# A transformer layer on one core: a new written-out order of work, with first and last rounds in an order of their own

## The reference

```
xn = layernorm(x)
Q, K, V = xn W_Q + b_Q, xn W_K + b_K, xn W_V + b_V       # 16 heads of 64
attn    = softmax(Q K^T / sqrt(64))                      # 256 x 256 for each head
x1 = x + layernorm(sum over heads (attn V) W_O + b_O)
gate = softmax(x1n gate_w^T), x1n = layernorm(x1)        # 8 experts
f  = x1n weight^T + (1/16) sum_e gate_e (x1n U_e^T) V_e^T  # rank 16 each
out = x1 + layernorm(f)
```

## Time and profile before

| what | value |
|---|---|
| median of 3 runs | 1220.18 us |
| profiled execution | 1221.85 us, its span 1220.0 us |
| PE busy | 1185.9 us, 97% of the span, 10532 matmuls |
| DVE, ACT, POOL busy | 958.6, 967.9 and 728.3 us |
| granted TensorE clock, mean | 0.99 of 2.4 GHz |

### The profile page before, as it was taken

One profiled execution on the slowest core, in us unless ns is written; L12 is line 12 of the kernel. 1 busy time (PEld: TensorE's weight loads), 2 busy tenths in 40 slices (PEclk: granted clock), 3 DMA queues, 4 the chain that ended last, 5 costly groups with the idle time before them and its releaser, 6 DMA issues.

```text
span 1220.0 us, 32981 instructions
## 1 busy us (share of the span) xinstructions
PE 1185.9 (97%) x10532; PEld 977.1 (80%) x10532; DVE 958.6 (79%) x2618; ACT 967.9 (79%) x3079; POOL 728.3 (60%) x946
## 2 busy tenths in 40 slices
PE   6899999999999999999999999999999999999995
PEld 3688888888888888888888888888888888888883
DVE  4677888887888887887877878877888878788883
ACT  2678888888888888888888888888888888888882
POOL 2556556665556665566665666675556665555653
PEclk9899999999999999999999999999999999999997
DMA  6000000000000000000000000000000000000000
GB/s 213 2 1 6 2 6 4 4 4 4 0 4 4 4 4 4 0 4 4 4 4 4 4 0 4 4 4 4 4 0 4 4 4 4 4 0 4 4 4 9
DMA packets 9923, 10.95 MB, mean 9 GB/s; under 512 B 816, under 2 KB 9392, under 8 KB 9904
## 3 DMA queue, kind: packets, MB, share of 16 engines
q1 hardware_dynamic: 9904, 10.70, 2.7%
HBM read 6.50 MB, written 4.19 MB: 9 GB/s over the span
## 4 chain that ended last, share of the span: by engine, by line
PE 82%; POOL 7%; DVE 6%; issue 4%; ACT 1%; POOLq 0%; DVEq 0%; DMA 0%; SPq 0%; ACTq 0%
PE o_ps L383 17%; PE st_ps L365 17%; PE st_ps L355 14%; PE extra_ps L398 8%; PE qk_ps L304 4%; PE qk_ps L306 4%; PE qk_ps L305 4%; POOL probs L1021 3%; PE extra_ps L337 3%; PE extra_ps L339 2%; PE extra_ps L338 2%; DVE probs_t L806 2%; PE extra_ps L270 2%; POOL xn L1010 1%; POOL xn L1015 1%
## 5 line engine op out<-in xcount | busy, mean ns | idle before, releaser
L1021 POOL TENSOR_TENSOR probs<-probs,inv_sum 128x512 f32<-128x512 f32 x512 | 525.4, 1042 | 352.6 <-DVE inv_sum L801 342.0
L563 ACT ACTIVATE probs<-st_ps,neg_max 128x256 f32<-128x256 f32 x1024 | 475.2, 482 | 102.6 <-DVE neg_max L794 99.7
L794 DVE TENSOR_REDUCE neg_max<-st_ps 128x2 f32<-128x512 f32 x512 | 332.0, 680 | 48.8 <-PE st_ps L355 45.7
L365 PE MATMUL st_ps<-ident,probs 128*128 128x128 f32 x2048 | 286.6, 275 | 6.7 <-POOL probs L1021 5.1
L365 PEld LDWEIGHTS st_ps<-ident,probs 128*128 128x128 f32 x2048 | 233.9, 141 | 46.9 <-POOL probs L1021 21.6
L383 PE MATMUL o_ps<-probs_t,v_sb 128*64 128x256 f32 x2048 | 256.3, 387 | 0.3 <-DVE o_lo L812 0.2
L563 ACT ACTIVATION_READ_ACCUMULATOR probs<-st_ps,neg_max 128x1 f32 x1024 | 217.1, 212 | 0.0
L806 DVE COPY probs_t<-st_ps 128x512 f32<-128x512 f32 x256 | 169.4, 683 | 37.4 <-PE st_ps L365 37.3
L383 PEld LDWEIGHTS o_ps<-probs_t,v_sb 128*64 128x64 f32 x2048 | 133.4, 136 | 73.2 <-issue 5.9
L778 DVE TENSOR_TENSOR qk_lo<-qk_ps,qk_hi 128x512 fp32r<-128x512 f32 x256 | 175.1, 684 | 11.8 <-ACT qk_hi L550 11.5
L571 ACT COPY probs_t<-st_ps 128x512 f32<-128x512 f32 x256 | 152.5, 596 | 32.6 <-PE st_ps L365 32.6
(11 more groups left out here) (116 smaller groups left out, 2073.4 us busy)
## 6 DMA issues: line engine op xcount, KB each, us to landing
out<-x_all SPq DMA_DIRECT2D x32, 128.0 KB, 1.7
x_all<-in_x SPq DMA_DIRECT2D x1, 3840.0 KB, 17.3
stage_v<-in_w_v SPq DMA_DIRECT2D x1, 512.0 KB, 4.1
stage_o<-in_w_o SPq DMA_DIRECT2D x1, 512.0 KB, 6.7
stage_q<-in_w_q SPq DMA_DIRECT2D x1, 384.0 KB, 4.7
stage_k<-in_w_k SPq DMA_DIRECT2D x1, 384.0 KB, 5.8
x_all<-in_x SPq DMA_DIRECT2D x2, 128.0 KB, 3.1
ffn<-in_ffn_w SPq DMA_DIRECT2D x1, 196.0 KB, 6.8
```

The costliest lines, as they stand in the source:

```text
L365: last = nc.tensor.transpose(st_ps[p % 2][h][:, s * T + j * P:s * T + (j + 1) * P], probs[p % N_PROBS][h][:, j, s * P:(s + 1) * P], ident[ ...
L563: last = nc.scalar.activation(probs[n][h][:, j, :], st_ps[p % 2][h][:, j * T:(j + 1) * T], ACT.Exp, bias=neg_max[n][h][:, j:j + 1], accum_ ...
L794: nc.vector.tensor_reduce(neg_max[p % N_PROBS][h][:, :], st_ps[p % 2][h][:, :].rearrange("p (j s) -> p j s", j=NT), AX.X, ALU.max, negate= ...
L1021: nc.gpsimd.tensor_tensor(probs[n][h][:, :, :], probs[n][h][:, :, :], inv_sum[n][h][:, :].unsqueeze(2).to_broadcast([P, NT, T]), ALU.mult) ...
```

## The change

It does these things:

- A new order of the calls in `body` on all four engines. On TensorE a round becomes: scores 6, values 2, values 3; scores 7; scores 0, values 4, values 5; scores 1; a transposes call, then values 6, values 7, scores 2; scores 3 (between output projections 1 and 2); scores 4, values 0, values 1; scores 5, with 128*128 work between these groups. The last `project_v` moves behind `transpose_x1`.
- The first three rounds and what follows the loop are no longer `body` with holes, but lists of their own (145 calls on TensorE ahead of the loop, 26 behind it). The loop still runs 29 rounds.
- v is no longer centred by TensorE. Its column sums give `v_offset`, and v's bias goes through the output projection into the bias b_O (`output_bias`: 9 matmuls of one column; `ffn_means`: 8 matmuls of one column instead of one). `MEANS` has 6 pieces instead of 8, and POOL builds no diagonals for v.
- 12 warm-up matmuls of 128x128 at the start, and a small ScalarE copy of `one` before the weights.
- On DVE `stats_x(2)` now stands in the first list between `fold_means(3)` and `fold_means(4)`.

```diff
+WARM_UPS = 12
@@
         def run(engine, lag, body):
-            for i in range(lag + 1):
-                body(i)
             with engine.Fori(0, B - 1 - lag) as step:
                 body(step + (lag + 1))
-            for i in range(B, B + lag):
-                body(i)
@@ TensorE
+            def warm_up():
+                for _ in range(WARM_UPS):
+                    nc.tensor.matmul(st_ps[1][1][:, 0:P], mean_w[:, :], mean_w[:, :], start=True, stop=True)
+            def ffn_means():
+                pe.wait_ge(mean_folded, 5)
+                pe.wait_ge(ffn_rows_centred, 1)
+                nc.tensor.matmul(o_ps[:, 0:D + TG], mean_w[:, :], ffn[:, F_W:F_W + D + TG],
+                                 start=True, stop=True)
+                pe.wait_ge(w_loaded["v"], 16)
+                for pair in range(PAIRS):
+                    last = nc.tensor.matmul(o_ps[:, D + TG + pair:D + TG + pair + 1],
+                                            stage["v"][:, pair_cols(pair)], one[:, 0:1],
+                                            start=True, stop=True)
+                last.then_inc(ffn_means_projected, 1)
+            def output_bias():
+                ...
+                nc.tensor.matmul(dst, neg_mean_w[:, :], bias[:, B_O:B_O + 1], start=True, stop=False)
+                for pair in range(PAIRS):
+                    last = nc.tensor.matmul(dst, stage["o"][:, pair_cols(pair)], v_offset[:, pair:pair + 1],
+                                            start=False, stop=(pair == PAIRS - 1))
@@ TensorE, the first list, its beginning
+            warm_up()
+            weight_means(0)
+            transpose_xn(0)
+            weight_means(1)
+            weight_means(2)
+            project_v(0, 0, free=(xt_lo_ready, 1))
+            weight_means(3)
+            project_qk(0, 0)
+            weight_means(4)
+            project_qk(0, 1)
+            weight_means(5)
+            project_v(0, 1, free=(v_copied[0], 1))
+            ffn_means()
+            project_v(0, 2, free=(v_copied[1], 1))
+            scores(0, 0)
+            scores(0, 1)
+            project_qk(0, 2, free=(qk_lo_ready, 1))
+            project_qk(0, 3, free=(qk_lo_ready, 2))
+            output_bias()
+            transpose_probs(0, 0, 0, free=(exp_ready[0], 1))
+            ...
@@ TensorE, body(i) (the waits left out here: each call has its free= as in the list above)
+                transpose_xn(i)
+                scores(i - 1, 6)
+                probs_v(i - 1, 2); probs_v(i - 1, 3)
+                project_tg(i - 2)
+                project_qk(i, 0)
+                transpose_probs(i - 1, 5, 1); transpose_probs(i - 1, 5, 0)
+                project_qk(i, 1)
+                transpose_probs(i - 1, 6, 0)
+                scores(i - 1, 7)
+                project_v(i, 0)
+                project_qk(i, 2)
+                transpose_probs(i - 1, 6, 1)
+                project_qk(i, 3)
+                project_v(i, 1)
+                scores(i, 0)
+                probs_v(i - 1, 4); probs_v(i - 1, 5)
+                project_qk(i, 4)
+                transpose_u(i - 2)
+                transpose_probs(i - 1, 7, 0); transpose_probs(i - 1, 7, 1); transpose_probs(i, 0, 0)
+                project_z(i - 2)
+                scores(i, 1)
+                transpose_probs(i, 0, 1)
+                probs_v(i - 1, 6); probs_v(i - 1, 7)
+                scores(i, 2)
+                project_v(i, 2)
+                transpose_probs(i, 1, 0)
+                project_qk(i, 5)
+                transpose_probs(i, 1, 1)
+                output_projection(i - 1, 0); output_projection(i - 1, 1)
+                scores(i, 3)
+                output_projection(i - 1, 2)
+                transpose_probs(i, 2, 1)
+                output_projection(i - 1, 3)
+                transpose_probs(i, 2, 0)
+                project_qk(i, 6)
+                transpose_y(i - 1)
+                scores(i, 4)
+                probs_v(i, 0); probs_v(i, 1)
+                project_qk(i, 7)
+                transpose_x1(i - 1)
+                transpose_probs(i, 3, 0); transpose_probs(i, 3, 1)
+                project_v(i, 3)
+                transpose_probs(i, 4, 1); transpose_probs(i, 4, 0)
+                scores(i, 5)
@@ DVE, the first list, its beginning
+            stats_x(0)
+            norm_first_x()
+            stats_x(1)
+            fold_means(0)
+            weight_lo("v", every, w_hi_ready, w_lo_ready)
+            fold_means(1)
+            weight_lo("q", early, early_hi_ready, early_lo_ready)
+            xt_low(0)
+            weight_lo("k", early, early_hi_ready, early_lo_ready)
+            fold_means(2)
+            w_o_means()
+            centre_ffn_rows()
+            fold_means(3)
+            stats_x(2)
+            fold_means(4)
+            qk_lo(0, 0)
+            weight_lo("q", late, w_hi_ready, w_lo_ready)
+            weight_lo("o", every, w_hi_ready, w_lo_ready)
+            fold_means(5)
+            qk_lo(0, 1)
+            centre_ffn_columns()
+            weight_lo("k", late, w_hi_ready, w_lo_ready)
+            row_max(0, 0, 0)
+            ...
@@ TensorE, behind the loop, its end
+            probs_v(31, 6, free=(o_lo_ready, 127))
+            transpose_probs(31, 7, 0, free=(exp_ready[0], 256))
+            output_projection(31, 0, free=(z_copied, 31))
+            output_projection(31, 1)
+            output_projection(31, 2)
+            probs_v(31, 7)
+            output_projection(31, 3)
+            transpose_y(31, free=(yt_ready, 32))
+            ...
```

More of the change, by code:

```diff
@@ L307, in project_qk, with project_v @@
                 last.then_inc(qk_projected, 1)
[L308 to L328, removed]
+            def project_v(b, quarter, free=None):
                 if first(b) and quarter == 0:
@@ new lines, in _ @@
+            project_qk(1, 3, free=(qk_lo_ready, 10))
+            probs_v(0, 4, free=(o_lo_ready, 2))
+            probs_v(0, 5)
+            transpose_probs(0, 6, 0, free=(exp_ready[0], 7))
+            transpose_probs(0, 6, 1, free=(exp_ready[1], 7))
+            transpose_probs(0, 7, 0, free=(exp_ready[0], 8))
+            project_v(1, 2, free=(v_copied[1], 2))
+            transpose_probs(0, 7, 1, free=(exp_ready[1], 8))
+            scores(1, 0, free0=(probs_t_copied[0], 7), free1=(probs_t_copied[1], 7))
@@ new lines, in _ @@
+            project_qk(1, 7, free=(qk_lo_ready, 14))
+            probs_v(1, 0, free=(o_lo_ready, 4))
+            probs_v(1, 1)
+            scores(1, 4, free0=(probs_t_copied[0], 11), free1=(probs_t_copied[1], 11))
+            transpose_x1(0, free=(x1_ready, 1))
+            transpose_probs(1, 3, 1, free=(exp_ready[1], 12))
+            project_v(1, 3, free=(x1t_ready, 1))
+            transpose_probs(1, 3, 0, free=(exp_ready[0], 12))
+            probs_v(1, 2, free=(o_lo_ready, 5))
+            probs_v(1, 3)
@@ new lines, in _ @@
+            transpose_probs(1, 4, 1, free=(exp_ready[1], 13))
+            transpose_probs(1, 4, 0, free=(exp_ready[0], 13))
+            transpose_xn(2, free=(v_copied[3], 2))
+            scores(1, 5, free0=(probs_t_copied[0], 12), free1=(probs_t_copied[1], 12))
+            scores(1, 6, free0=(probs_t_copied[0], 13), free1=(probs_t_copied[1], 13))
+            probs_v(1, 4, free=(o_lo_ready, 6))
+            project_tg(0, free=(xt_lo_ready, 3))
+            project_qk(2, 0, free=(qk_lo_ready, 15))
@@ new lines, in _ @@
+            transpose_probs(2, 0, 1, free=(exp_ready[1], 17))
+            project_v(2, 2, free=(z_copied, 1))
+            probs_v(1, 6, free=(o_lo_ready, 7))
+            probs_v(1, 7)
+            scores(2, 2, free0=(probs_t_copied[0], 17), free1=(probs_t_copied[1], 17))
+            project_qk(2, 5, free=(qk_lo_ready, 20))
+            project_qk(2, 6, free=(qk_lo_ready, 21))
+            output_projection(1, 0, free=(v_copied[2], 3))
+            transpose_probs(2, 1, 0, free=(exp_ready[0], 18))
@@ new lines, in _ @@
+            probs_v(2, 0, free=(o_lo_ready, 8))
+            probs_v(2, 1)
+            transpose_probs(2, 3, 1, free=(exp_ready[1], 20))
+            transpose_x1(1, free=(x1_ready, 2))
+            transpose_probs(2, 3, 0, free=(exp_ready[0], 20))
+            project_v(2, 3, free=(x1t_ready, 2))
+            transpose_probs(2, 4, 1, free=(exp_ready[1], 21))
+            transpose_probs(2, 4, 0, free=(exp_ready[0], 21))
+            scores(2, 5, free0=(probs_t_copied[0], 20), free1=(probs_t_copied[1], 20))
@@ L685, in _ @@
-            run(act, 2, body)
+            nc.scalar.copy(seen_one[:, :], one[:, :])
+            weight_hi("v", every, w_hi_ready)
+            weight_hi("q", early, early_hi_ready, 1)
+            xt_high(0)
+            weight_hi("k", early, early_hi_ready, 2)
+            copy_v(0, 0)
+            qk_hi(0, 0)
+            weight_hi("q", late, w_hi_ready, 4)
+            weight_hi("o", every, w_hi_ready)
+            qk_hi(0, 1)
+            copy_v(0, 1)
+            weight_hi("k", late, w_hi_ready, 6)
@@ new lines, in _ @@
```

(17 more changed lines are left out.)

1089 lines of the change are left out of this document (717 added, 372 removed).

## The result

The changed kernel took 1232.61 us (median of 4 runs, 1232.06 to 1233.45) against 1220.13 us for the kernel before (4 runs, 1218.62 to 1221.35). The ratio is 1.0103, with a 95% interval of 1.0086 to 1.0121: slower by 12.5 us. The forecast was 1229.0, range 1219 to 1240.

The account below looks back on a forecast made before the run. TensorE's own sequence was taken to bound the loop, with waits mattering only at both ends. Median 1220.18 us, plus 14.8 (loop), minus 6 (ahead), 0 (behind), gave 1229.0 us; range 1219 to 1240.

Parts of the forecast that it names:

- The loop, +14.8 forecast: 29 loop rounds, each +0.78 us for 20 changes of shape instead of 16 and -0.27 for a removed wait for POOL.
- the places without a row: In the loop, scores before a projection (three times, 0.20 us each) and values 7 before scores 2 (0.19).
- the 0.12 of the loop's edge: Last transposes to values: 0.92 us in a loop round, 0.80 in a written-out one; the 0.12 was forecast to stay.
- the places that I called even to within 0.2 us: In the loop, project_v(i, 3) behind copy_x1t, transposes 3/0 and norm_x behind POOL: priced 0, range 0 to 0.3 us a round.
- rival 1: New waits in the loop: one place late by 0.3 us each round, +8.7 us, 1238 us; chance 0.17.
- Ahead of the loop, -6 forecast: Stretch before the loop: 4.6 us and 3.5 us gained, 2.0 lost to 11 more shape changes; from -2 to -14.
- Its first half: Ahead of the loop: load lands at 22.9, first row maximum 30.1, first transposes about 34.4 against 38.27; 4.6 us gained.
- The second half, 3.5 us from better filled rounds 1 and 2: Ahead of the loop, behind the first transposes: better filled rounds win 3.5 us of idle time and low clock.
- Behind the loop, 0 forecast: After the loop: some 2 us won, against uncovered copies behind values 7 and seven more shape changes; 0, give or take 1.5.
- 2 (the ends gain 14 us): Both ends gain all they can, load hidden or early, holes filled: +14.8 - 14 = +0.8, 1221 us; chance 0.12.
- 3 (unshown places are free): In the loop, four places no loop row shows cost nothing, 0.8 us off each round; with ends -14, 1206 us; chance 0.07.
- 4 (the surcharge hides a wait): Shape-change surcharge is time TensorE waits anyway; the loop only loses its wait: -14, 1206 us; chance 0.04.

Follow-up runs that it names:

- Experiment 1: Kernel before with project_qk(i, 1) moved between scores 6 and scores 7: 1249.68 us, ratio 1.0233.
- experiment 2: Kernel before with project_qk(i, 1) between scores 6 and 7 and project_qk(i, 6) between scores 4 and 5: 1249.35 us, ratio 1.0236.
- values_in_twos: Kernel before with values 0 moved right ahead of values 1, behind scores 4 and 5: 1230.42 us, ratio 1.0078.
- xn_ahead: Kernel before with transpose_xn moved ahead of transpose_probs(i, 4, 0): 1213.18 us, ratio 0.9936.
- experiment 9: Kernel before with an unused tile of 32 bytes a partition behind `one`, no instruction changed: 1224.45 us, ratio 1.0021.
- 3: Kernel before with values 0 moved right ahead of values 1, the same run as values_in_twos: 1230.42 us, ratio 1.0078.
- 6: Changed kernel with transpose_probs(i, 0, 1) moved ahead of scores(i, 1): 1260.42 us, ratio 1.0331.
- 11: Kernel before with transpose_xn ahead of transpose_probs(i, 4, 0), values 0 beside values 1, project_v(i, 3) and project_qk(i, 6) ahead of transposes: 1235.32 us, ratio 1.011.
- transpose_ahead: Changed kernel with transpose_probs(i, 0, 1) moved ahead of scores(i, 1), the same run as 6: 1260.42 us, ratio 1.0331.
- no_warm_up: Changed kernel without the 12 warm-up matmuls: 1231.92 us.
- experiment 8: Changed kernel with stats_x(2) later, transpose_probs(i, 0, 1) ahead of scores(i, 1), and values 7 ahead of the last output projections 0 to 2: 1252.77 us, ratio 1.027.
- experiment 5: Changed kernel with stats_x(2) moved on DVE to right ahead of the first row maximum: 1225.63 us, ratio 1.0043 to the kernel before.
- experiment 10: Kernel before with transpose_xn moved ahead of transpose_probs(i, 4, 0), the same run as xn_ahead: 1213.18 us, ratio 0.9936.
- pad_alone: Kernel before with an unused tile of 32 bytes a partition, the same run as experiment 9: 1224.45 us, ratio 1.0021.

## Why the prediction was right, and where it was not

**The loop, +14.8 forecast, +10.9 measured.** The mechanism is the forecast one and is shown: the same work, TensorE without a wait, 20 changes of shape instead of 16. Experiment 1 gave 0.39 us for two of them and experiment 2 0.34 for two more, each apart from the waits. The values I chose for the places without a row (0.20 and 0.19) came out at 0.20 and 0.19, and these rows agree with the rule of the Trainium skill, page "TensorEngine Tiling (Array Packing)", section Tiling Modes, that a change of tiling mode drains TensorE.

**The size.** A round came to 36.75, where 36.38 + 0.78 - 0.27 is 36.89. The count is not at fault (`project_tg` makes it 0.83, and the gap larger). The step that was mis-sized is what I left in place: the 0.12 of the loop's edge, which I said stays. It is gone. `transpose_xn` stands behind scores at the edge now and takes 0.37 us, just what two transposes behind scores took in the middle of a round of before, so nothing but the exit of 0.15 is paid there. The old order without its wait says the same: in values_in_twos the calls at the edge are those of before, and the last transposes and `transpose_xn` start 0.43 and 0.31 us ahead of what follows them, 0.74 together, where I had read 0.92 in a loop round and 0.80 in a written-out one:

```profile
644.37 0.60 PE L365 MATMUL st_ps<-ident,probs 128*128 128x128 f32 x4
644.80 0.38 PE L270 MATMUL extra_ps<-ident,xn 128*128 128x128 f32 x2
645.11 1.08 PE L383 MATMUL o_ps<-probs_t,v_sb 128*64 128x256 f32 x8
```

So the 0.12 went with the wait and is no price of the edge as such. (In xn_ahead 0.1 of it is still there, 1.67 us from the last projection's start to the values against 1.57 in a written-out round; why is open.) Another 0.08 stood at scores 3 before values 0, a group of 0.89 from start to start where others have 0.81. It was in the chain of before and I didn't read it, 1.69 us for 24 matmuls where the earlier trace rows has 1.63:

```profile
623.90 1.69 PE st_ps L355 x24
```

It is gone with its place, and was nothing of the count. With both, 36.38 + 0.83 - 0.27 - 0.12 - 0.08 is 36.74. That it meets 36.75 so well is in part chance, since the changed kernel's tiles can hold a shift like that of experiment 9 (last section).

**The waits in the loop.** None of the places that I called even to within 0.2 us turned into a wait. But experiments 1, 2, 3, 6 and 11 show how near they were: each moved one to four calls and lost 0.5 to 1.1 us a round to a wait in another place. That the changed order has none is a property of the order as a whole; rival 1 had much for it.

**Ahead of the loop, -6 forecast, -0.55 measured.** This step failed. Its first half was right: the wait for the load (landing at 21.9, forecast 22.9) and the first row maximum at 30.61 (30.1). The first transposes came at 35.66 instead of 34.4, because I had left out that TensorE falls to 1.2 GHz behind the wait: scores 0 and 1 took 1.4 us each there, and the 16 records of eight single-column matmuls 3.4. (For all sixteen such matmuls I had written some 2 us, where 16 x 0.2 is already 3.2; from start to start they took 3.3 at half clock and 1.8 at full.) The second half, 3.5 us from better filled rounds 1 and 2, was a guess and is refuted: from the first transposes to the loop it takes 92.6 us instead of 90.5, although the clock from 36 to 60 us is 1.00 instead of 0.88. These lists have waits of their own:

```profile
PE extra_ps L263 <- DVE x L1072: 1.5, 1, 1.5
PE extra_ps L423 <- issue: 1.3, 1, 1.3
PE extra_ps L340 <- DVE x1t L1112: 0.9, 1, 0.9
...
```

That is TensorE's list of waits from 36 to 128 us without its last line (0.8 for POOL); the sum is 4.5 us. The three shown belong to batch 0's small chain through `extra_ps`; before, the same stretch (38 to 129) waited 3.8 us. The rest of the 2.1 us is not told apart; the 11 added changes of shape were priced at 2.0. How exact the -0.55 is: the profiles of the changed kernel, transpose_ahead and no_warm_up start the loop at 128.25, 126.73 and 127.00, the first two with the same lists, so one profile tells it to some 1.5 us. The clock accounts for that: behind the wait for the load it is at 0.50 for 10.2 us in the first of these profiles and for 6.8 us in the other two, and 3.4 us at half speed cost up to 1.7.

**Behind the loop, 0 forecast, +1.3 measured**, within the 1.5 given. The uncovered copies behind values 7 are the reason for 0.9 of it (experiment 8).

**The total** was nearer than its terms, by luck: the loop was forecast 3.9 too high, the two ends 6.8 too low together, and the errors cancel in part.

**The rivals.** 1 (new waits in the loop) fell: 0.4 us of idle TensorE in 29 rounds. 2 (the ends gain 14 us) fell; experiment 5 shows that the load's wait was worth 6 to 7 us. 3 (unshown places are free) is refuted by the rows of after. 4 (the surcharge hides a wait) is refuted by experiments 1 and 2, and by a loop with no wait in which all 20 are paid.

## What to carry to other kernels

Where TensorE is never idle, read its chain call by call: the cost of a call depends on what stands before it, and here 0.14 to 0.20 us are paid at each change between full (128*128), row-tiled (64*128) and column-tiled (128*64) use. A new order is first counted in such changes, and a wait that it removes is worth little more than its own length (here 0.27 to 0.38 us of 36.4). But the count alone is no guide: five of the six reorderings of the loop that were run (all but experiment 10) opened waits of 0.5 to 1.1 us a round elsewhere, because each call also covers a chain of the other engines. The edit that paid (0.64% faster) filled the one wait with a call whose input the trace showed ready. In a list that engines work in order, a step that waits for the largest load goes behind all that can do without it.

## What the runs showed of the hardware that I had not expected

An unused tile of 32 bytes a partition made the same instructions slower by 0.09 us a round, 0.2% of the kernel. It is in the matmuls: two of the three kinds of the output projection have a mean duration of 282 and 281 ns with the tile and 279 and 279 without, in the kernel before and in xn_ahead alike. The groups of instructions between 200 and 1100 us (busy us, mean ns), first in the kernel before:

```profile
L398 PE MATMUL extra_ps<-o_lo,wo_hi 128*128 128x256 f32 x193 | 53.8, 279 | 0.0
L398 PE MATMUL extra_ps<-o_hi,wo_lo 128*128 128x256 f32 x193 | 53.8, 279 | 0.0
```

And in pad_alone:

```profile
L399 PE MATMUL extra_ps<-o_lo,wo_hi 128*128 128x256 f32 x192 | 54.2, 282 | 0.0
L399 PE MATMUL extra_ps<-o_hi,wo_lo 128*128 128x256 f32 x192 | 53.9, 281 | 0.0
```

The changed kernel adds small tiles too, and has 280 and 282 ns there, so its round of 36.75 can hold part of such a shift; how much was not tried. Comparisons below 0.3% between kernels with different tiles can hold such a shift.
